# Keys and values of all batches first, attention of both halves in one run, output projection as a pass of its own

## The reference

```python
q = layernorm(x) @ Wq ; k = ctx @ Wk ; v = ctx @ Wv     # heads 32, 8, 8
q, k = q * cos + rotate_half(q) * sin, k * cos + rotate_half(k) * sin
scores = where(mask == 0, -1e9, q @ k.T / sqrt(128))    # four query heads share one key head
x = x + (softmax(scores) @ v) @ Wo
W = scales * (unpack4(qweight) - zeros)                 # 1024 x 1024
out = x + layernorm(x) @ W + bias
```

## Time and profile before

| what | value |
| --- | --- |
| median of 3 runs | 2573.49 us (2572.2 to 2575.67) |
| span of the profiled execution | 2571.3 us |
| TensorE busy in it | 2491.1 us, 97% |
| VectorE busy | 1730.0 us, 67% |
| ScalarE busy | 1051.5 us, 41% |
| GpSimd busy | 692.8 us, 27% |
| data moved by DMA | 234.82 MB, mean 91 GB/s |

### The profile page before, as it was taken

The page is one execution under the profiler, slowest core; times in us unless marked ns, Lnnn a source line. Parts: engine busy times, 40 slices in busy tenths (PEclk is TensorE's granted clock), DMA queues, the critical chain, the costliest instruction groups (busy, mean ns, idle before and its releaser), DMA issues.

```text
span 2571.3 us, 39372 instructions
## 1 busy us (share of the span) xinstructions
PE 2491.1 (97%) x12960; PEld 2108.8 (82%) x12960; DVE 1730.0 (67%) x3078; ACT 1051.5 (41%) x2418; POOL 692.8 (27%) x376
## 2 busy tenths in 40 slices
PE   8999999999999999998989999999999999999989
PEld 6777888888888888886777778888888888888867
DVE  4885666766776767667249857766677677676671
ACT  3124544444444445442032244454444444544420
POOL 1441222222222222214114412222222222222241
PEclk9999999999999999999999999999999999999999
DMA  8553222222222222211465532222222212222111
GB/s 266 171 179 100 89 66 65 65 67 91 70 66 73 65 78 77 65 58 50 142 195 182 167 117 66 66 65 65 84 79 65 73 65 70 85 65 65 58 50 66
DMA packets 202519, 234.82 MB, mean 91 GB/s; under 512 B 10968, under 2 KB 138200, under 8 KB 202456
## 3 DMA queue, kind: packets, MB, share of 16 engines
q1 hardware_dynamic: 199384, 223.52, 27.3%
q10 hardware_dynamic: 2304, 8.39, 0.8%
q0 software_dynamic: 768, 2.10, 0.3%
HBM read 183.64 MB, written 50.33 MB: 91 GB/s over the span
## 4 chain that ended last, share of the span: by engine, by line
PE 86%; DVE 7%; issue 3%; DMA 2%; ACT 1%; SPq 0%; POOL 0%; DVEq 0%; ACTq 0%; POOLq 0%
PE ps L228 27%; PE ps L229 27%; PE ps L230 27%; PE ps L560 4%; DVE probs L932 2%; PE ps L415 1%; DVE parts L789 1%; DVE probs L935 1%; DVE rope_tmp L802 1%; DVE rope_tmp L804 1%; DMA scores<-in_L_ffn_scales 1%; DVE probs L851 1%; DMA raw<-in_L_xattn_Wk 0%; DMA raw<-in_L_xattn_Wo 0%; DMA rope_tmp<-in_L_xattn_Wv 0%
## 5 line engine op out<-in xcount | busy, mean ns | idle before, releaser
L1071 POOL TENSOR_TENSOR parts<-raw,parts 128x1024 fp32r<-128x1024 f32 (+1 forms) x176 | 422.9, 2404 | 945.7 <-ACT parts L634 945.5
L228 PE MATMUL ps<-act_t,parts 128*128 128x512 f32 x1280 | 503.2, 393 | 15.3 <-DVE parts L789 14.7
L229 PE MATMUL ps<-act_t,parts 128*128 128x512 f32 x1280 | 499.8, 390 | 0.0
L230 PE MATMUL ps<-act_t,parts 128*128 128x512 f32 x1280 | 498.2, 389 | 0.0
L228 PE MATMUL ps<-parts 128*128 128x512 f32 x1024 | 426.3, 416 | 17.8 <-DVE rows L964 13.6
L715 ACT ACTIVATE probs<-scores,neg_max 128x256 f32<-128x256 f32 x512 | 254.3, 497 | 429.5 <-DVE neg_max L983 429.5
L1076 POOL TENSOR_TENSOR rope_tmp<-rope_tmp 128x512 f32<-128x512 f32 x160 | 209.6, 1310 | 751.4 <-DVE rope_tmp L804 751.1
L230 PE MATMUL ps<-parts 128*128 128x512 f32 x1024 | 405.4, 396 | 0.0
L229 PE MATMUL ps<-parts 128*128 128x512 f32 x1024 | 404.1, 395 | 0.0
L964 DVE TENSOR_TENSOR rows<-ps,rows 128x512 f32<-128x512 f32 x512 | 351.7, 688 | 27.7 <-PE ps L230 11.5
L228 PEld LDWEIGHTS ps<-act_t,parts 128*128 128x128 f32 x1280 | 240.9, 188 | 73.2 <-DVE parts L789 27.1
(11 more groups left out here) (83 smaller groups left out, 4279.5 us busy)
## 6 DMA issues: line engine op xcount, KB each, us to landing
raw<-in_L_xattn_Wq SPq DMA_DIRECT2D x64, 512.0 KB, 5.1
parts<-k_scratch SPq DMA_DIRECT2D x64, 512.0 KB, 4.6
parts<-v_scratch SPq DMA_DIRECT2D x64, 512.0 KB, 5.4
raw<-in_L_xattn_Wo SPq DMA_DIRECT2D x64, 512.0 KB, 5.7
v_scratch<-parts SPq DMA_DIRECT2D x64, 256.0 KB, 2.8
k_scratch<-parts SPq DMA_DIRECT2D x64, 256.0 KB, 2.9
rows<-in_ctx SPq DMA_DIRECT2D x16, 512.0 KB, 4.9
raw<-in_L_xattn_Wk SPq DMA_DIRECT2D x16, 512.0 KB, 4.9
```

The lines of the kernel that those rows point to most:

```text
L228: eng.matmul(dst, lh, rh, start=(k == 0), stop=False)
L229: eng.matmul(dst, lh, rl, start=False, stop=False)
L230: last = eng.matmul(dst, ll, rh, start=False, stop=(k == n - 1))
L1071: pool.tensor_tensor(dst, raw[i % 2][:, 0:a * c].rearrange("p (a c) -> p a c", a=a), hi.bitcast(F32), ALU.subtract).then_inc(raw_split, 1)
```

## The change

The loop over halves is gone from the outside; stages now cover both halves one after the other.

- The context, positions and weights are laid out by the host in the order in which they are read: `ctx_4096` transposed in tiles of 128 x 128 blocks, `Wq` and `Wk` by head, `Wv` in blocks. No context tile is transposed on the chip.
- Stage A makes all keys and values: 64 units in the order V (half 0, first columns), K (half 0), V (half 0, second columns), V (half 1, second), K (half 1), V (half 1, first). The statistics of all 16 tiles of x are taken in K of half 0, and the x tiles of half 0 are turned in the last V stage. The rotation tables of the halves are kept in scratch memory.
- Stage B is attention: 16 groups of one key head and 8 units; a unit is one batch and two query heads. Four units belong to a pair. A unit of TensorE has the scores of the next unit, the weighted values of the last one (512 columns, both heads at once), half of the query products for a unit three later, the transposes, and the other half. Query low parts and Wq low parts are GpSimd's now. The output goes to scratch memory (`left_scratch`) in float32. In group 7 the tiles of x of half 1 are normalized and turned (`x_fill`, four in each of units 2 to 5, all in bank `BK_X`).
- Stage C is the output projection: 8 products (`MS`) of 16 steps (`PAIRS`); a step reads 1024 rows of one head's output and 128 x 512 of Wo, splits both, and adds 24 products into the eight banks. Two such sets of 16 steps make a block of 8 tiles and 512 columns, which VectorE adds to the rows of x. The 4-bit weight is unpacked in steps 7 to 14.
- The dense layer follows for 16 tiles, with both column halves of a tile together.

Attention scores are scaled when the key is split and no longer in the exponential.

```diff
+V_H0_N0, K_H0, V_H0_N1, V_H1_N1, K_H1, V_H1_N0 = 0, 8, 24, 32, 40, 56
...
@@ SyncE, keys of half 0 @@
+            for u in range(16):
+                g = u // 2
+                if u + 2 < 2 * TT:
+                    load_x(u, u + 2, (ln_chain, 2 * u + 2))
+                if u % 2 == 1:
+                    load_head(g + 2, wk[(g + 2) % KVH])
+                if u in (2, 4, 6, 8):
+                    load_ring(C_WV1 + u // 2 - 1)
+                store_unit(K_H0 + u)
...
@@ VectorE, keys of half 0 @@
+            for u in range(16):
+                key_rot(K_H0 + u, u)
+                key_lo(K_H0 + u)
+                x_stats(u)
+                if u % 2 == 1:
+                    head_lo(u // 2 + 2)
+                if u in (3, 5, 7, 9):
+                    ring_lo(C_WV1 + (u - 3) // 2)
+            inverse_std(0, 0, 2 * TT)
...
@@ SyncE, keys of half 1 @@
+            for u in range(16):
+                g = u // 2
+                if u % 2 == 1:
+                    i = KVH + g + 2
+                    load_head(i, wk[i - KVH] if i < 2 * KVH else wq[i - 2 * KVH])
+                if u in (0, 2, 4, 6):
+                    load_ring(C_WV0 + u // 2)
+                store_unit(K_H1 + u)
...
@@ TensorE, attention @@
+            def attention(G, first=False, switch=False, last=False):
+                for u8 in range(UPG):
+                    i, pair = u8 % 4, G * 2 + (u8 // 4 + 1)
+                    more = not (last and u8 >= 4)
+                    fills = []
+                    if switch and 2 <= u8 < 6:
+                        fills = [2 * TT + 4 * (u8 - 2) + f for f in range(4)]
+                    if u8 < UPG - 1:
+                        score(G, u8 + 1)
+                    elif not last:
+                        score(G + 1, 0)
+                    if fills:
+                        x_fill(fills[0], BK_X)
+                    if u8 > 0:
+                        weigh(G, u8 - 1, first=first and u8 == 1)
+                    elif not first:
+                        weigh(G - 1, UPG - 1)
+                    if fills:
+                        x_fill(fills[1], BK_X)
...
+                    if more:
+                        query(pair, i, 0, G * UPG + (u8 + 4))
+                    if fills:
+                        x_fill(fills[2], BK_X)
+                    turn(G, u8, first=first and u8 == 0)
+                    if more:
+                        query(pair, i, 1, G * UPG + (u8 + 4))
+                    if fills:
+                        x_fill(fills[3], BK_X)
...
@@ VectorE, attention @@
+                    if not (last and u8 >= 5):
...
+                        query_rot((u8 + 3) % 4, G * UPG + (u8 + 3))
...
+                        masked(nG, nxt, nh)
+                    if switch and 2 <= u8 < 6:
+                        for f in range(2 * TT + 4 * (u8 - 2), 2 * TT + 4 * (u8 - 2) + 2):
+                            fill_lo(f, BK_X)
+                    if not (last and u8 == UPG - 1):
+                        inverse_sum(nG, nxt)
...
+                    if switch and u8 in (1, 2, 3, 4):
+                        x_normalize(2 * (u8 - 1), 1)
+                        x_normalize(2 * (u8 - 1) + 1, 1)
...
@@ SyncE, group 7; the load waits for the transposes of the tile two before @@
+                        if u8 in (2, 3, 4):
+                            load_x_again(2 * (u8 - 1), 1)
+                            load_x_again(2 * (u8 - 1) + 1, 1)
...
@@ TensorE, projection @@
+            for m in range(MS):
+                block_step(m, 0, m * PAIRS, 0)
+                with pe.Fori(0, 7) as h:
+                    block_step(m, None, h * 2 + (m * PAIRS + 1), 1)
+                    block_step(m, None, h * 2 + (m * PAIRS + 2), 0)
+                block_step(m, PAIRS - 1, m * PAIRS + PAIRS - 1, 1)
...
@@ SyncE, projection @@
+            sp.dma_start(packed, qweight).then_inc(dense_in, 16)
...
+            for s in range(2, STEPS):
+                load_step(s)
+                if s - 2 < 16:
+                    r = s - 2
+                    sp.dma_start(rows[:, r, :], x_rows[row_tile(r)]).then_inc(rows_in[r // 8], 16)
...
@@ VectorE, projection @@
+                step_lo(s)
...
+                if 7 <= s < 15:
+                    dense_full(s - 7)
+                    dense_lo(s - 7)
```

More of the change, by code:

```diff
@@ new lines, in x_fill @@
+            def x_fill(f, bank):
+                t = f // 2
+                pe.wait_ge(x_norm, t + 1)
+                if f < 2:
+                    pe.wait_ge(tb_cos, 8)
+                    pe.wait_ge(tb_sin, 8)
+                else:
+                    pe.wait_ge(x_lo, f - 1 if f < 2 * TT else f)
+                for i in range(4):
+                    k = 4 * (f % 2) + i
+                    mm = pe.transpose(ps[:, bank, i * P:(i + 1) * P], xring[t % 2][:, k * P:(k + 1) * P], identity[:, :])
+                mm.then_inc(x_done, 1)
@@ new lines, in _ @@
+            for c in range(2):
+                dve.wait_ge(rope_in[c], 16)
+            query_rot(0, 0, first=True)
+            query_rot(1, 1)
+            query_rot(2, 2)
+            masked(0, 0, 0)
+            inverse_sum(0, 0)
+            attention(0, 0, first=True)
+            with dve.Fori(1, 7) as G:
+                attention(G, 0)
+            attention(7, 0, switch=True)
+            with dve.Fori(8, 15) as G:
+                attention(G, 1)
+            attention(15, 1, last=True)
@@ new lines, in rope_sum, with fill @@
+            def rope_sum(wait, value, done):
+                pool.wait_ge(wait, value)
+                pool.tensor_tensor(rope_tmp[:, 0, :], rope_tmp[:, 0, :], rope_tmp[:, 1, :], ALU.add).then_inc(done, 1)
+            pool.wait_ge(idx_ready, 1)
+            gather(0)
+            pool.wait_ge(tb_done, 4)
+            gather(1)
+            for u in range(16):
+                rope_sum(k_rot, u + 1, k_sum)
+            for u in range(16):
+                rope_sum(k_rot, 16 + u + 1, k_sum)
+            def fill(b, half, wait=None):
+                if wait is not None:
+                    pool.wait_ge(*wait)
+                pool.memset(score_v[:, b, :, :], MASKED).then_inc(fill_done, 1)
@@ new lines, in attention @@
+            def attention(G, first=False, switch=False, last=False):
+                for u8 in range(UPG):
+                    b = u8 % 4
+                    if not (last and u8 >= 5):
+                        rope_sum(q_rot, G * UPG + (u8 + 4), q_sum)
+                        query_lo((u8 + 3) // 4 % 2, (u8 + 3) % 4, G * UPG + (u8 + 3))
+                    if b == 0 and not (last and u8 == 4):
+                        head_lo(1, G * 4 + (2 * (u8 // 4) + 20))
+                    if b == 3 and not last:
+                        head_lo(0, G * 4 + (2 * (u8 // 4) + 21))
+                    if switch and u8 >= 4:
+                        fill(b, 1, (exp_done, 2 * (60 + b) + 2))
@@ new lines, in _ @@
+            pool.wait_ge(c_lo, C_WV0 + 4)
+            pool.wait_ge(tb_done, 8)
+            for b in range(HB):
+                fill(b, 0)
+            for m in range(3):
+                rope_sum(q_rot, m + 1, q_sum)
+                query_lo(0, m, m)
+            head_lo(0, 19)
+            attention(0, first=True)
+            with pool.Fori(1, 7) as G:
+                attention(G)
+            attention(7, switch=True)
+            with pool.Fori(8, 15) as G:
+                attention(G)
```

1837 lines of the change are left out of this document (954 added, 883 removed).

## The result

The changed kernel takes 2632.84 us (median of 4 runs, 2629.06 to 2635.48) against 2572.84 (4 runs, 2572.05 to 2575.67) for the kernel before on the same chip: a ratio of 1.0228, 95% interval 1.0213 to 1.0242. It is 2.3% slower. The profiled execution has a span of 2630.4 us, 59 more than before.

The account below looks back on a forecast made before the run. TensorE's stream of products plus its interruptions was taken to bound the kernel: 2434 us of stream and small gaps plus the stage losses made a 2628 us span, 2630 for the median run, range 2588 to 2680.

Parts of the forecast that it names:

- keys of half 0: First half's key stage: VectorE's serial passes and late head loads on odd units make TensorE lose 70 us.
- Keys of half 1: Second half's key stage: no statistics, but head loads issued late behind stores; 15 us lost (8 to 20).
- stream and small gaps: TensorE's products and transposes over the whole kernel, 2419.1 us, plus 15 for small gaps of quiet stretches: 2434.
- value stages: Stages making the values: VectorE needs some 2.5 us of each 5.45 us unit; nothing lost, 1 us allowed.
- attention units: Repeated units of attention: TensorE's 9.1 us of work covers the other engines; nothing lost.
- switch: Second half's x inside attention, group 7 iterations 2 to 5: waits for fills and x loads, 44 us (30 to 52).
- tail and start of projection: Last four attention units without queries, 11 us; projection steps 0 and 2 waiting for operands, 10 us (5 to 14).
- unpacking: Projection steps 7 to 14: VectorE needs 8.0 us a step beside GpSimd's passes; 18 us lost (7 to 27).
- rival 1: Key stages do not bind, as loads land ahead of head_lo; 85 less, 2545 us; chance 0.10.
- Rival 4: The switch is cheap, 15 instead of 44 us, with the rest as forecast: 2601 us; chance 0.08.
- Rivals 2 and 3: Projection steps bound by conversion and load, 2690 us; attention bound by ScalarE and in-order hand-overs, 2694; chance 0.10 each.
- rival 3: Attention bound by ScalarE and in-order hand-overs, 9.6 us a unit: 64 more, 2694 us; chance 0.10.

Follow-up runs that it names:

- the buffer alone: Changed kernel with a third buffer for the x tiles of half 1, order kept: 2627.52 us, ratio 1.0209.
- buffer with order: Changed kernel with the third x buffer and the x fills of group 7 reordered: 2605.64 us, ratio 1.0124.
- the mends: Changed kernel with early head loads in both key stages, moved statistics, spread unpacking, steps 2 and 3 loaded first, third x buffer, new fill order: 2508.94 us, ratio 0.9748.

## Why the prediction was right, and where not

The time fell 3 us from the forecast of 2630, and the direction and the largest places are shown by the runs. The signs that the prediction named came too: VectorE stood 7.6 us at `head_lo` where it had 6, the keys of half 0 lasted 156.5 us (near 155), iterations 3 to 5 of group 7 lasted 23.2 to 23.4 (over 20), and quiet units and steps 9.15 and 5.44. Keys of half 1, with 96.3, and TensorE's busy share in the keys of half 0, 66% in the window shown and not 55%, were off; slow products count as busy. The terms, in us; measured is what TensorE's start distances in a stage have over the products' steady distances, for which windows stand above:

| term | predicted | measured |
| --- | --- | --- |
| stream and small gaps | 2419 + 15 | 2419 + 5 (what is left over) |
| start | 11 | 12 |
| keys of half 0 | 70 | 72 |
| keys of half 1 | 15 | 9 |
| value stages | 1 | 8 |
| start of attention | 8 | 8.5 |
| attention units | 0 | 0 |
| switch | 44 | 43.5 |
| tail and start of projection | 21 | 25 |
| steps | 0 | 0 |
| unpacking | 18 | 23.5 |
| dense start and end | 6 | 5 |

That the sum came within 3 us is in part luck: terms too small by 20 us together met terms too large by 17.

- **The stream was right.** Busy time and 100% windows agree with 2419 to a few us; the 15 for small gaps were too much.
- **Keys of half 0 were right in cause and size.** Both ingredients, the load behind the issue order and the serial passes, were confirmed by an edit each (50 and 23 us off the stage), and the distances of the rotations, 5.9 and 13.6 to 15.9, stand against 6.1 and 14.0 to 15.2 predicted. The 3 us lost at the start of the values behind are in the 72. The load was dearer than taken: these seven landed in a median of 5.6 us, each issued 0.4 us behind a load of x, and not in 4.9 (DMA issues of the window 57 to 215). The two key stages cost 81 where rival 1 had 28 or none; it falls.

```profile
wraw<-in_L_xattn_Wk SPq DMA_DIRECT2D x7, 512.0 KB, 5.6
```

- **Keys of half 1 were mis-sized.** The step "odd units take 7.8" took the landing of 4.9 from the earlier trace rows; in this stage the six loads of Wk have a median of 3.9 (DMA issues of the window 300 to 405):

```profile
wraw<-in_L_xattn_Wk SPq DMA_DIRECT2D x6, 512.0 KB, 3.9
```

  From rotation to rotation the odd units took 7.0 to 7.1 us (7.8 to 8.2 with a `ring_lo`) where 7.8 and 9.0 were costed; 0.8 less in eight of them takes 15 to near 9. Issuing the load a unit earlier takes 5 off these 9.
- **"The value stages ... nothing, 1 us allowed" failed.** The last value stage turns the first x tiles, and VectorE stands 3.4 us for their load, with a TensorE gap of 3.0 behind it:

```profile
416.11 0.81 DVE L1010 TENSOR_SCALAR xring<-xring,mean_var,inv_std 128x1024 f32<-128x1024 f32 x1 [3.41 <-DMA xring<-in_x]
```

  I had costed VectorE's work there and not the load ahead of it. This error, 7 up, and that of the keys of half 1, 6 down, nearly cancel.
- **The switch was right as a sum and wrong in its parts.** "It stands some 5 us while TensorE goes on" was 2.15 us in the iteration shown and 1.9 to 2.4 in all three; the order made up for it, as the buffer alone (6 us) and buffer with order (29 us) show. The walk had some 16 us for the load and 28 for the rest. Each iteration's loss was close to the walk's (6, 12, 12.5 and 12.5 against 7, 12, 13 and 12), so the sizes were right for a cause that was only partly so. Rival 4 falls: 43.5, not 15.
- **Unpacking: the rate was right, the lead and the clock were not.** The eight shifts (L1175) start between 1753.6 and 1808.8, 7.9 us apart, against 8.0 predicted. In the window 1760 to 1842 the 259 products need 59 us at 0.227; of the 23 lost, 14 are idle and 9 are products at a granted clock of 0.88. The sum had eight steps of 2.55 over the products less 2.5 of lead, 18. By the starts, step 15 comes 64.5 us behind step 7, 20.9 over the products: the rate without any lead, for the first gap opens at step 8. Slow products behind the last gap add 2.5. How much of the other slow products only filled time in which VectorE would have been waited for was not tried. Of the prices between which I had chosen, 6.6 a step with nobody in the way and 9.1 with all of GpSimd's pass waited out, neither held: a pass collides in one step and not in another (last section). The tail and the start of the projection, at a clock of 0.78, came out 4 over their sum.
- **Rivals 2 and 3 fall.** A quiet unit of attention has room for a ScalarE pass that takes 0.52 us of its time, and the steps for twice the left operand's traffic. But three passes cost 79 us, 0.6 a unit: the "0" of attention was nearer to a cliff than my walk said, and rival 3's 9.6 was some 1.4 us of ScalarE work away.

Where the change's own gain went: the stream is 23 us shorter, and interruptions rose from 130 (2571.3 - 2441.7) to 211 (2630.4 - 2419.1). With the mends they are 86 (2504.7 - 2419.1), below before's. So with good orders the restructuring gains 23 + 44 = 67 us, and the orders and the two x buffers that it came with cost 126.

## What to carry to other kernels

When an engine's instruction waits for a load, look in the queue for what stands ahead of that load, above all a load that waits for the same engine's work of the same iteration: the two then add up in every iteration, and moving one issue line gives it back. When a gap names a late transfer, walk on to what the next engine does after it arrives, since a buffer does not help where the consumer's order is what is late. And cost a gap together with the clock behind it: in the four short stages, with gaps of 2 to 9 us and a granted clock of 0.78 to 0.88, the slow products behind the gaps come to 0.3 to 0.6 of the idle time again.

## What was not expected of the hardware

In a projection step VectorE's difference of 128 x 512 (L1159) takes a mean of 2345 ns, and a difference of the same shape with one operand in PSUM (L1132) takes 686. Groups of the changed kernel by line, with count, busy us, mean ns and the idle time before:

```profile
L1159 DVE TENSOR_TENSOR b_parts<-wraw,b_parts 128x512 fp32r<-128x512 f32 x128 | 300.0, 2345 | 339.4 <-ACT b_parts L886 339.3
L1327 POOL TENSOR_TENSOR a_parts<-xring,a_parts 128x1024 fp32r<-128x1024 f32 x128 | 309.8, 2420 | 437.5 <-ACT a_parts L884 437.5
...
L1132 DVE TENSOR_TENSOR probs_t<-ps,probs_t 128x512 fp32r<-128x512 f32 x256 | 164.9, 686 | 116.6 <-ACT probs_t L856 116.6
```

The timeline shows it beside GpSimd's pass:

```profile
1760.08 0.68 DVE L1159 TENSOR_TENSOR b_parts<-wraw,b_parts 128x512 fp32r<-128x512 f32 x1
...
1761.62 3.26 POOL L1327 TENSOR_TENSOR a_parts<-xring,a_parts 128x1024 fp32r<-128x1024 f32 x1 [2.54 <-ACT a_parts L884]
...
1762.66 3.30 DVE L1180 TENSOR_TENSOR v_c<-v_c 128x1024 f32<-128x1024 f32 x1
...
2100.76 2.40 POOL L1327 TENSOR_TENSOR a_parts<-xring,a_parts 128x1024 fp32r<-128x1024 f32 x1 [3.04 <-ACT a_parts L884]
...
2101.23 2.48 DVE L1159 TENSOR_TENSOR b_parts<-wraw,b_parts 128x512 fp32r<-128x512 f32 x1 [2.97 <-ACT b_parts L886]
```

With GpSimd idle the pass takes 0.68; started 0.5 us into GpSimd's, it ends 0.55 us after it (2103.71 and 2103.16). The later pass L1180, whose operands both lie in SBUF too, does the same, with 3.30 us here and 1.22 in a step where GpSimd is idle. Over the whole trace the 7 differences of L1159 that meet no GpSimd pass take 681 ns, and the 121 that do a mean of 2441. Those of L1132 with one operand in PSUM take 686 in either case, though 116 of the 256 lie wholly beside a GpSimd pass. So it is the second SBUF operand and GpSimd's pass together that cost the time, and neither alone. The Trainium skill (SBUF — State Buffer, Who interferes with whom) says that a VectorE operation with two SBUF inputs contends with a GpSimd one that reads SBUF, for a port pair that only one of them holds at a time. The trace agrees, with 2441 ns against 681. Here it cost nothing in quiet steps, where VectorE has 5.45 us for it.

Most loads of 512 KB landed in 3.4 to 4.1 us after issue, against the 4.9 of the earlier trace rows (KB each, median us):

```profile
xring<-left_scratch SPq DMA_DIRECT2D x128, 512.0 KB, 3.4
wraw<-in_L_xattn_Wq SPq DMA_DIRECT2D x64, 512.0 KB, 3.9
...
xring<-in_x SPq DMA_DIRECT2D x32, 512.0 KB, 4.1
```

The seven of Wk in the keys of half 0 took 5.6. Why the others are shorter was not tried.
